# Attention and a graph product on one core: the prelude's copies, scales and keys in another order, and queries split two units ahead

## The chip, the cores and the metric

The kernel runs on one core of a Trainium2 chip. The metric is the device time of one execution in microseconds (us). TensorE multiplies matrices into PSUM (eight banks of 512 float32 in each of 128 partitions), VectorE and ScalarE work element by element, GpSimd and SyncE issue transfers (DMA). Each engine runs its own instructions in order and waits on semaphores.

## The reference

```python
q, k, v = x @ Wq.T + bq, key @ Wk.T + bk, value @ Wv.T + bv      # 4096 x 512 each
scores = (q @ k.T) / 4096 ** 0.5 * adj                           # 4096 x 4096
scores = where(abs(scores) < 1e-5, -1e9, scores)
x1 = layernorm(x + (softmax(scores) @ v) @ Wm.T + bm)
out = layernorm(x1 + relu((adj @ x1) @ W.T + b))
```

## The kernel before

**Numbers.** Products in float32 quality are made of float16 (or float32r) halves: each operand is split into a high half, written by ScalarE, and a low half, what is left, written by VectorE; each product has three passes (high by high, low by high, high by low). Operands are first multiplied by a power of two: `up[:, S_K]` for keys, `up[:, S_V]` for values, `up[:, S_T]` for queries, `up[:, S_W]` for the weights of the values.

**Folding.** q @ k.T is computed as (x A + bq Wk) key.T plus a term for each query row, with A = Wq.T Wk, and Wv and Wm are multiplied into one matrix (Wvm). So "queries" below are t = x A + b, called t, 32 tiles of 128 rows.

**Prelude.** TensorE makes A (L773), the rows of the biases (L756), turns Wm (L787), turns the first rows of x (L765) and multiplies Wv by Wm (L802). ScalarE copies in the order: Wq and Wk, biases, Wv (L1091), A out of PSUM (L1094), Wm. VectorE makes the low halves in the same order (L1350, L1371, L1382), with the rows of the biases (L1375 to L1379) ahead of Wm's. SyncE has loaded Wq and Wk, x's first rows, Wm and Wv; GpSimd issues the loads of 2048 keys (L669) once the last part of Wk is in.

Then come eight groups G of four tiles. For each e of 0 to 3, TensorE turns a tile of x for group G + 1 (`x_turn`, banks 0 and 1), in groups 4 to 6 turns a tile of 128 keys in bank BK = 2 (`key_turn`, L831; the next turn waits for the low half, L1442), and makes 128 columns of the group's queries in bank BT + e, BT = 4 (`queries`, L818). ScalarE writes x's high half (L1075), the key's (L1119) and copies the queries to `tq` (L1113), which GpSimd stores in `t_dram`. VectorE makes the low halves (L1343, L1442), the largest magnitudes of keys and values, one chunk of 512 rows at a time (`chunk_maximum`, L1403; the staging buffers `stg` are loaded anew by GpSimd, L659, when a chunk has been read), and of the queries (`t_maximum`, L1408, `last_t_maximum`, L1414). A scale is made in steps: `scale_square` (L1420, L1423) spreads the maxima of the partitions over a square `gsq`, TensorE turns it (`scale_turn`, L825), and `scale_made` (L1427 to L1438) makes the power of two. S_W is made at the start of group 2, S_K of group 4, S_V of group 6, S_T after group 7. The raw Wvm is split after its scale (L1141, L1473). The last four key tiles (KEYS_AFTER) are turned after group 7, in one bank; VectorE makes their low halves before `scale_made(S_T)`.

**Units.** A unit g is one tile of queries by one half of the keys: 32 units for each half. TensorE makes its scores (`scores`, L857, 48 matmuls in four banks BS + c) and weights the values with its probabilities (`weigh`, L877, 48 matmuls). VectorE adds and masks the scores (L1535, which frees the bank), ScalarE takes magnitudes (L1168), VectorE sets small ones to -1e9 and takes the maximum, ScalarE makes exponentials (L1173) and the high probabilities (L1181), VectorE the low ones (L1564), and SyncE turns both by DMA (L375, L378) into `PT`, which `weigh` reads. The tile of t for unit g + 1 is loaded (`load_t`, L350) and split (`t_high`, L1158; `t_low`, L1508) in the step of unit g, so `scores(g + 1)` waits for it. `thl` has two buffers. The output of a unit of the first half is copied (`copy_first`, L1186) and stored (`store_first`).

The order of TensorE is written out: scores 0, 1, weigh 0, scores 2, weigh 1, scores 3, weigh 2, then loops of scores(g), weigh(g - 1). After the second half's units come products with adj (L972, L1004).

Of the kernel before, what the change touches and what calls it, by code (L numbers as in the profile page):

```python
# [21 lines left out]
P_SCALE = 2.0 ** 14  # L22

# [18 lines left out]
def attention_then_aggregation(nc, x, adj, key, value, wq, bq, wk, bk, wv, bv, wm, bm, w1, b1, out):  # L42
# [40 lines left out]
    with ctx:  # L83
# [10 lines left out]
        tcol = sb(ctx, "tcol", [P, NG + KD - 1], fp32)  # L94
# [101 lines left out]
        with ExitStack() as prep:  # L196
# [9 lines left out]
            bq_k = sb(prep, "bq_k", [P, KD, 1], fp32)  # L206
            bcol = sb(prep, "bcol", [P, 3, KD], fp32)
# [43 lines left out]
        t_mm, t_ev, t_mx = sem("t_mm"), sem("t_copied"), sem("t_maxima")  # L251
# [57 lines left out]
        KEYS_AFTER = (12, 13, 14, 15)  # L309

# [12 lines left out]
        with nc.Block() as block:  # L323

            @block.sync
            def _(sp):
# [44 lines left out]
                def turn_prob(g, b):  # L371

                    scales_made()
# [29 lines left out]
                def first_step(g, b, j):  # L403

                    nb, nj = 1 - b, j + b
                    load_t(g + 1, g + 1)
# [4 lines left out]
                    if not isinstance(g, int) or g >= 1:  # L411
                        store_first(g - 1, g - 1, 1 - b)
# [22 lines left out]
                with sp.Fori(1, NT // 2 - 1) as i:  # L435
                    for b in range(2):
                        first_step(2 * i + b, b, i)
# [4 lines left out]
                load_t(g + 1, 0)  # L442
# [72 lines left out]
                def second_step(n, b, j, merged, rows, products, copied=False, sums=False, copies=False):  # L515

                    g = NT + n
                    if not isinstance(n, int) or n < NT - 1:
                        load_t(g + 1, n + 1)
# [36 lines left out]
                load_t(NT + 1, 1)  # L556
# [86 lines left out]
            def _(pool):  # L643
# [23 lines left out]
                pool.wait_ge(s_w[KD - 1], 32)  # L667
# [84 lines left out]
            def _(pe):  # L752
# [45 lines left out]
                pe.wait_ge(s_rout, 4)  # L798
# [10 lines left out]
                def queries(G, e):  # L809
# [4 lines left out]
                    wait(pe, t_ev, KD * (G - 1) + e + 1)  # L814
# [12 lines left out]
                def key_turn(m):  # L827
                    pe.wait_ge(key_in[m // TC], 16)
                    wait(pe, k_lo, m)
                    for k in range(KD):  # L830
                        last = nc.tensor.transpose(ps[:, BK, k * P:(k + 1) * P], keyn[:, m, k * P:(k + 1) * P], ident[:, :])  # L831
# [86 lines left out]
                scores(1, 1, 0)  # L918
                weigh(0, 0, 0)
                scores(2, 0, 0)  # L920
# [150 lines left out]
            def _(act):  # L1071
# [34 lines left out]
                def t_out(G, e):  # L1106
                    b = G % 2
                    act.wait_ge(t_mm, KD * G + e + 1)
                    if G >= 2:

                        act.wait_ge(t_st[b], 16 * (G // 2))
                        act.wait_ge(t_mx, G - 1)
# [956 lines left out]
```

## Time and profile before

| | before |
|---|---|
| time, median of 3 runs (lowest to highest) | 2096.1 us (2095.8 to 2097.22) |
| the profiled execution: time / span | 2098.29 us / 2096.6 us |
| TensorE busy | 2044.8 us, 98% of the span |
| VectorE / ScalarE / GpSimd busy | 1466.7 / 676.3 / 81.5 us |
| mean share of full TensorE clock granted | 0.989 |
| scores (L857) / weighted values (L877) | 676.5 / 673.5 us |
| the queries' products (L818) | 97.0 us |

The span runs from the first to the last instruction of one profiled execution; the time of that execution also holds what lies around them. A line of the timeline gives start, duration, engine, line of the kernel, operation, out<-in, shapes, and in brackets how long the engine had stood idle before it and what released it.

### The profile page before, as it was taken

How to read it: one execution, taken by the hardware profiler on the slowest of the kernel's cores; microseconds unless marked ns; L12 is line 12 of the kernel's file. 1: busy time of each engine (PE TensorE's matmuls, PEld its weight loads, DVE VectorE, ACT ScalarE, POOL GpSimd, SP SyncE). 2: the span in 40 equal slices, each digit the busy share in tenths (PEclk: the TensorE clock that was granted, in tenths of full speed). 3: DMA queues.
4: the chain of work that ended last, by engine and by line, in shares of the span. 5: the costliest groups of instructions: out<-in, count | busy, mean ns of one | idle time of the engine just before them, and what ended most of it. 6: DMA issues, size and time to landing. Idle time of an engine off the chain costs nothing.

```text
span 2096.6 us, 29772 instructions
## 1 busy us (share of the span) xinstructions
PE 2044.8 (98%) x9471; PEld 980.8 (47%) x9471; DVE 1466.7 (70%) x3354; ACT 676.3 (32%) x884; POOL 81.5 (4%) x139
## 2 busy tenths in 40 slices
PE   7987999999999999999999999999999999999998
PEld 6873444444444444444444444444444444444443
DVE  3876656565666656587777777778888757887887
ACT  3343434343434344343333333334444210000000
POOL 1110000000000000000000000000000000000000
PEclk9998999999999999999999999999999999999999
DMA  7675886767677766788666666777777996455551
GB/s 246 216 281 147 194 184 144 177 154 178 151 174 157 173 158 164 208 177 182 161 160 161 161 162 162 168 171 182 180 180 210 229 266 148 126 121 120 135 134 61
DMA packets 586673, 359.56 MB, mean 171 GB/s; under 512 B 501376, under 2 KB 505472, under 8 KB 586240
## 3 DMA queue, kind: packets, MB, share of 16 engines
q1 hardware_dynamic: 565056, 275.07, 52.5%
q0 software_dynamic: 21568, 83.89, 16.4%
q8 instruction: 24, 0.39, 0.1%
q14 instruction: 25, 0.20, 0.0%
HBM read 181.15 MB, written 88.60 MB: 129 GB/s over the span
## 4 chain that ended last, share of the span: by engine, by line
PE 93%; DVE 3%; DMA 2%; SPq 1%; ACT 1%; issue 0%; DVEq 0%; ACTq 0%
PE ps L857 31%; PE ps L877 31%; PE ps L1004 16%; PE ps L912 4%; PE ps L898 4%; PE ps L818 3%; PE ps L972 2%; DMA wc<-in_L_gnn_Wv 1%; PE ps L802 1%; DMA x1T<-x1hl 1%; PE ps L765 0%; DMA stg<-in_L_gnn_value 0%; PE ps L831 0%; DVE mcol L1403 0%; DVE tcol L1408 0%
## 5 line engine op out<-in xcount | busy, mean ns | idle before, releaser
L857 PE MATMUL ps<-KT,thl 128*128 128x512 f16 x3072 | 676.5, 380 | 9.9 <-DVE thl L1508 9.9
L877 PE MATMUL ps<-V,PT 128*128 128x512 f16 x3072 | 673.5, 379 | 0.6 <-issue 0.6
L857 PEld LDWEIGHTS ps<-KT,thl 128*128 128x128 f16 x3072 | 301.1, 98 | 375.2 <-DVE thl L1508 11.3
L877 PEld LDWEIGHTS ps<-V,PT 128*128 128x128 f16 x3072 | 300.4, 98 | 363.5 <-issue 1.9
L1535 DVE SCALAR_TENSOR_TENSOR prob<-ps,c_now,adjh 128x512 f32<-128x512 f32 x256 | 192.1, 751 | 288.4 <-PE ps L857 287.6
L1168 ACT ACTIVATE small<-prob 128x512 f32<-128x512 f32 x256 | 161.8, 632 | 629.5 <-DVE prob L1535 342.5
L1564 DVE SCALAR_TENSOR_TENSOR Phl<-prob,Phl 128x2048 f16<-128x2048 f32 x64 | 146.7, 2292 | 77.3 <-ACT Phl L1181 77.1
L1548 DVE CUSTOM_DVE_ANT_0 prob<-prob,small 128x512 f32<-128x512 f32 x256 | 174.4, 684 | 0.0
L1173 ACT ACTIVATE prob<-prob,nbias,inv 128x2048 f32<-128x2048 f32 x64 | 134.2, 2097 | 95.1 <-DVE nbias L1557 95.1
L1541 DVE TENSOR_SCALAR small<-small,eps_s,neg_s 128x512 f32<-128x512 f32 x256 | 139.2, 544 | 21.0 <-ACT small L1168 21.0
L1181 ACT ACTIVATE Phl<-prob 128x2048 f16<-128x2048 f32 x64 | 122.4, 1912 | 7.1
L1331 ACT ACTIVATE p<-ps 128x512 f32<-128x512 f32 x14 | 8.4, 598 | 332.1 <-PE ps L1004 332.1
L1004 PE MATMUL ps<-Y,AT 128*128 128x512 f16 x448 | 99.0, 379 | 0.0
L818 PE MATMUL ps<-xT,Aq 128*128 128x512 f32 x384 | 97.0, 403 | 1.8 <-DVE xT L1343 1.8
L912 PE MATMUL ps<-W1T,x1T 128*128 128x512 f16 x384 | 91.3, 389 | 5.3 <-DMA x1T<-x1hl 5.3
L696 POOL DMA_DIRECT2D adjh<-in_adj x64 | 36.3, 568 | 1387.2 <-DMA adj_bf<-adjh 782.5
L898 PE MATMUL ps<-Wvm,UT 128*128 128x512 f16 x384 | 88.1, 379 | 0.2 <-issue 0.2
L1004 PE MATMUL ps<-Ta,S 128*128 128x512 f16 x336 | 79.4, 379 | 0.0
L1004 PE MATMUL ps<-Tb,S 128*128 128x512 f16 x336 | 79.4, 379 | 0.0
L818 PEld LDWEIGHTS ps<-xT,Aq 128*128 128x128 f32 x384 | 71.0, 191 | 16.6 <-DVE xT L1343 2.5
L1004 PEld LDWEIGHTS ps<-Y,AT 128*128 128x128 bf16 x448 | 43.8, 98 | 52.8
L912 PEld LDWEIGHTS ps<-W1T,x1T 128*128 128x128 f16 x384 | 38.2, 100 | 53.3 <-DMA x1T<-x1hl 6.3
(182 smaller groups left out, 1739.7 us busy)
## 6 DMA issues: line engine op xcount, KB each, us to landing
adjh<-in_adj POOLq DMA_DIRECT2D x64, 512.0 KB, 5.4
adj_bf<-adjh SPq DMA_DIRECT2D x64, 512.0 KB, 4.4
t_in<-t_dram SPq DMA_DIRECT2D x64, 256.0 KB, 2.9
x_in<-in_x SPq DMA_DIRECT2D x64, 256.0 KB, 4.2
stg<-in_L_gnn_value POOLq DMA_DIRECT2D x12, 1024.0 KB, 7.2
rows<-in_x SPq DMA_DIRECT2D x32, 256.0 KB, 3.7
t_dram<-tq POOLq DMA_DIRECT2D x8, 1024.0 KB, 8.9
o_dram<-z_out SPq DMA_DIRECT2D x32, 256.0 KB, 2.8
```

The costliest lines, as they stand in the source:

```text
L818: last = nc.tensor.matmul(ps[:, BT + e, :], Aq[:, m, k, e * P:(e + 1) * P], xT[:, b, s, k, :], start=(n == 0), stop=(n == 3 * KD - 1))
L857: last = nc.tensor.matmul(ps[:, BS + c, :], thl[:, b, s, k * P:(k + 1) * P], KT[:, m, k, c * C:(c + 1) * C], start=(n == 0), stop=(n == 3 ...
L877: last = nc.tensor.matmul(ps[:, BU + b, :], PT[:, b, s, m, :], V[:, v, m, :], start=(m == 0 and q == 0), stop=(m == MT - 1 and q == 2))
L898: last = nc.tensor.matmul(ps[:, BZ, :], UT[:, b, s, k, :], Wvm[:, m, k, :], start=(n == 0), stop=(n == 3 * KD - 1))
L912: last = nc.tensor.matmul(ps[:, BY, :].rearrange("p (o n) -> p o n", n=P), x1T[:, s, k, :], W1T[:, m, :, k, :], start=(q == 0), stop=(q == ...
L1004: last = nc.tensor.matmul(ps[:, bank, :].rearrange("p (s d) -> p s d", s=2), left(m), right(m), start=(m == 0), stop=(m == NP - 1))
L1168: nc.scalar.activation(small[:, c % 2, :], prob[:, b, c * C:(c + 1) * C], ACT.Abs).then_inc(s_abs, 1)
L1173: nc.scalar.activation(prob[:, b, :], prob[:, b, :], ACT.Exp, bias=nbias[:, b:b + 1], scale=inv[:, 0:1], accum_out=rsum[:, b:b + 1]).then_ ...
L1535: nc.vector.scalar_tensor_tensor(out=prob[:, b, c * C:(c + 1) * C], in0=ps[:, BS + c, :], scalar=c_now[:, b:b + 1], in1=adjh[:, b, c * C:( ...
L1541: nc.vector.tensor_scalar(small[:, c % 2, :], small[:, c % 2, :], eps_s[:, 0:1], neg_s[:, 0:1], ALU.is_lt, ALU.mult).then_inc(s_neg, 1)
L1548: nc.vector.tensor_tensor_reduce(out=prob[:, b, c * C:(c + 1) * C], in0=prob[:, b, c * C:(c + 1) * C], in1=small[:, c % 2, :], scale=1.0, ...
L1564: nc.vector.scalar_tensor_tensor(out=Phl[:, b, LO, :], in0=prob[:, b, :], scalar=P_SCALE, in1=Phl[:, b, HI, :], op0=ALU.mult, op1=ALU.subt ...
```

## The change

- The sums that make the queries' scale: behind each copy of queries, ScalarE takes the magnitude in place in PSUM, times 2^-9, and sums it over 512 columns into one column of `tcol` (32 columns instead of 11); the maximum of these sums makes the scale, with TOP x 2^-9. The maxima on VectorE are gone. TensorE waits for the sum and not for the copy before it writes the bank again. A second copy of the bias, times 2^-9, is made.
- ScalarE and VectorE take A out of PSUM before they split Wv. GpSimd waits for Wv instead of Wk before it loads keys.
- S_W is made two tiles later (group 2, tile 2), Wvm's high half one tile later, its low half at the start of group 3.
- The last four key tiles are turned into four banks, those of the queries; their low halves are made after the first unit's queries are split.
- A tile of t is loaded and split two units ahead: 0 and 1 at the start, then g + 2 in the step of unit g.
- TensorE makes the scores of units 0, 1 and 2 before it weighs unit 0. ScalarE copies the outputs of 0 and 1 behind its step of unit 2, and SyncE stores them there.

```diff
@@ SyncE
                 def first_step(g, b, j):
-                    load_t(g + 1, g + 1)
+                    load_t(g + 2, (g + 2) % NT if isinstance(g, int) else g + 2)
                     wait(sp, s_c, g)
...
-                    if not isinstance(g, int) or g >= 1:
+                    if isinstance(g, int) and g == 2:
+                        store_first(0, 0, 0)
+                    if not isinstance(g, int) or g >= 2:
                         store_first(g - 1, g - 1, 1 - b)
...
                 load_key(0, 0)
+                load_t(1, 1)
@@ GpSimd
-                pool.wait_ge(s_w[KD - 1], 32)
+                pool.wait_ge(s_wv, 16)
                 for q in range(MC):
                     pool.dma_start(keyn[:, q * TC:(q + 1) * TC, :], chunk(key, q)).then_inc(key_in[q], 16)
@@ TensorE
-                    wait(pe, t_ev, KD * (G - 1) + e + 1)
+                    wait(pe, t_mx, KD * (G - 1) + e + 1)
...
-                    wait(pe, k_lo, m)
+                    if m in KEYS_AFTER:
+                        pe.wait_ge(t_mx, KD * (NG - 1) + m - KEYS_AFTER[0] + 1)
+                    else:
+                        wait(pe, k_lo, m)
...
-                        if e == 0 and G in (2, 4, 6):
+                        if (G, e) in ((2, 2), (4, 0), (6, 0)):
                             scale_turn(G // 2 - 1)
...
                 scores(1, 1, 0)
+                scores(2, 0, 0)
                 weigh(0, 0, 0)
-                scores(2, 0, 0)
                 weigh(1, 1, 0)
@@ ScalarE
+                for d in range(KD):
+                    act.wait_ge(s_amm, d + 1)
+                    nc.scalar.activation(Aq[:, HI, d, :], ps[:, d, :], ACT.Copy, scale=SCALE).then_inc(s_ahi, 1)
                 act.wait_ge(s_wv, 16)
                 for e in range(KD):
                     nc.scalar.activation(wv_s[:, HI, e, :], wc[:, e, :], ACT.Copy).then_inc(s_whi, 1)
-                for d in range(KD):
-                    act.wait_ge(s_amm, d + 1)
-                    nc.scalar.activation(Aq[:, HI, d, :], ps[:, d, :], ACT.Copy, scale=SCALE).then_inc(s_ahi, 1)
...
                                          ACT.Identity, bias=bq_k[:, e, :]).then_inc(t_ev, 1)
+                    act.wait_ge(t_ev, KD * G + e + 1)
+                    nc.scalar.activation(ps[:, BT + e, :], ps[:, BT + e, :], ACT.Abs, bias=bq_d[:, e, :], scale=T_DOWN,
+                                         accum_out=tcol[:, KD * G + e:KD * G + e + 1]).then_inc(t_mx, 1)
...
-                        t_high(g + 1, 1 - b)
+                        t_high(g + 2, b)
@@ VectorE
-                        if G == 2 and e == 3:
+                        if G == 3 and e == 0:
                             dve.wait_ge(s_vhi, 1)
...
-                        if G > 0 and e == 2:
-                            t_maximum(G - 1)
...
-                        if G == NG - 1:
-                            last_t_maximum(e)
-                scale_square(S_T, tcol[:, :], t_mx, NG + KD - 1)
-                for m in KEYS_AFTER:
-                    key_low(m)
-                scale_made(S_T)
+                scale_square(S_T, tcol[:, :], t_mx, NG * KD)
+                scale_made(S_T, top=TOP * T_DOWN)
...
                 t_low(0, 0)
+                for m in KEYS_AFTER:
+                    key_low(m)
                 c_first(0, 0, 0, 0)
+                t_low(1, 1)
                 value_low(3)
...
-                    t_low(g + 1, 1 - b)
+                    t_low(g + 2, b)
```

## Rows read from the trace of the kernel before

**Rows 1.** Waits of TensorE over the span: us in total, times, longest.

```profile
PE ps L857 <- DVE thl L1508: 9.9, 3, 5.5
PE ps L787 <- DVE Aq L1371: 8.2, 1, 8.2
```

**Rows 2.** Timeline of all engines, 0 to 58 us.

```profile
6.20 13.37 PE L773 MATMUL ps<-wk_s,wq_s 128*128 128x512 f32 x48 [6.20 <-DVE wk_s L1350]
...
10.22 3.14 POOL L669 DMA_DIRECT2D keyn<-in_L_gnn_key  x4 [8.48 <-DMA wb<-in_L_gnn_Wk]
...
24.84 0.28 PE L781 MATMUL ps<-bb,ones 128*128 128x4 f32 x2
27.64 2.19 ACT L1091 ACTIVATE wv_s<-wc 128x512 fp32r<-128x512 f32 x4 [13.01 <-DMA wc<-in_L_gnn_Wv]
...
33.34 3.64 PE L787 MATMUL ps<-ident,wd 128*128 128x128 f32 x16 [8.22 <-DVE Aq L1371]
...
37.66 0.69 DVE L1382 TENSOR_TENSOR wmT_s<-ps,wmT_s 128x512 fp32r<-128x512 f32 x1 [0.16 <-ACT wmT_s L1097]
...
38.74 3.02 PE L802 MATMUL ps<-wmT_s,wv_s 128*128 128x512 f32 x12
```

**Rows 3.** TensorE by stretch: us, PE busy, granted clock, DMA share, GB/s.

```profile
10.00:20.00 10.00, 10.00 (x43) 1.00 0.97 335
```

**Rows 4.** Timeline of all engines, groups 2 to 4 of the prelude.

```profile
89.56 2.00 ACT L1141 ACTIVATE Wvm<-wvm_raw,up 128x2048 f16<-128x2048 f32 x1
...
92.69 2.34 DVE L1473 SCALAR_TENSOR_TENSOR Wvm<-wvm_raw,up,Wvm 128x2048 f16<-128x2048 f32 x1
...
95.55 2.28 DVE L1403 TENSOR_REDUCE mcol<-stg 128x1 f32<-128x2048 f32 x1
...
98.12 0.75 POOL L659 DMA_DIRECT2D stg<-in_L_gnn_value  x1 [10.06 <-DVE mcol L1403]
...
105.11 2.29 DVE L1403 TENSOR_REDUCE mcol<-stg 128x1 f32<-128x2048 f32 x1 [1.71 <-DMA stg<-in_L_gnn_value]
...
108.53 0.33 PE L825 MATMUL ps<-ident,gsq 128*128 128x128 f32 x1 [2.62 <-DVE gsq L1423]
```

**Rows 5.** Timeline of all engines, one tile of group 4.

```profile
117.30 0.69 ACT L1113 ACTIVATE tq<-ps,bq_k 128x512 f32<-128x512 f32 x1 [1.87 <-PE ps L818]
...
119.12 0.74 DVE L1442 SCALAR_TENSOR_TENSOR KT<-ps,up,KT 128x512 f16<-128x512 f32 x1
...
121.16 0.60 PE L831 MATMUL ps<-ident,keyn 128*128 128x128 f32 x4
```

**Rows 6.** Timeline of all engines, group 7 and the queries' scale.

```profile
156.94 11.20 PE L818 MATMUL ps<-xT,Aq 128*128 128x512 f32 x48 [1.57 <-DVE xT L1343]
...
178.88 0.28 DVE L1427 TENSOR_REDUCE gm<-ps 128x1 f32<-128x128 f32 x1
...
180.12 0.72 ACT L1158 ACTIVATE thl<-t_in,up 128x512 f16<-128x512 f32 x1 [1.95 <-DVE inv L1499]
```

**Rows 7.** Timeline of all engines, the first two units.

```profile
200.49 0.19 ACT L1173 ACTIVATION_READ_ACCUMULATOR prob<-prob,nbias,inv 128x1 f32 x1
...
204.93 0.74 DVE L1535 SCALAR_TENSOR_TENSOR prob<-ps,c_now,adjh 128x512 f32<-128x512 f32 x1
...
220.00 2.29 DVE L1564 SCALAR_TENSOR_TENSOR Phl<-prob,Phl 128x2048 f16<-128x2048 f32 x1 [1.77 <-ACT Phl L1181]
```

**Rows 8.** Timeline of TensorE alone, the first units.

```profile
181.75 12.14 PE L857 MATMUL ps<-KT,thl 128*128 128x512 f16 x48 [4.09 <-DVE thl L1508]
199.36 11.87 PE L857 MATMUL ps<-KT,thl 128*128 128x512 f16 x48 [5.47 <-DVE thl L1508]
211.16 10.52 PE L877 MATMUL ps<-V,PT 128*128 128x512 f16 x48
221.52 10.52 PE L857 MATMUL ps<-KT,thl 128*128 128x512 f16 x48
```

**Rows 9.** DMA of tile PT until 240 us, from issue to landing.

```profile
DMA to landing us min/median/max: 5.7/6.1/6.2
```

More of the change, by code:

```diff
@@ L22 @@
 P_SCALE = 2.0 ** 14
+T_DOWN = 2.0 ** -9
 X_UP = 2.0 ** 9
@@ L309, in attention_then_aggregation, with key_bank @@
         KEYS_AFTER = (12, 13, 14, 15)
+        def key_bank(m):
+            return BT + m - KEYS_AFTER[0] if m in KEYS_AFTER else BK
         def staged(use):
@@ L371, in turn_prob @@
                 def turn_prob(g, b):
+                    if not isinstance(g, int):
+                        sp.to_reg(g + 1)
                     scales_made()
@@ L434, in _ @@
                 sp.dma_start(w1_raw[:, :, :], w1.rearrange("(o p) e -> p o e", p=P)).then_inc(s_wm, 16)
-                with sp.Fori(1, NT // 2 - 1) as i:
+                for b in range(2):
+                    first_step(2 + b, b, 1)
+                with sp.Fori(2, NT // 2 - 1) as i:
                     for b in range(2):
@@ L517, in second_step @@
                     g = NT + n
-                    if not isinstance(n, int) or n < NT - 1:
-                        load_t(g + 1, n + 1)
+                    if not isinstance(n, int) or n < NT - 2:
+                        load_t(g + 2, n + 2)
                     store_adj(g, n, b, j, 1)
@@ L828, in key_turn @@
                     pe.wait_ge(key_in[m // TC], 16)
[L829 removed]
+                    if m in KEYS_AFTER:
+                        pe.wait_ge(t_mx, KD * (NG - 1) + m - KEYS_AFTER[0] + 1)
+                    else:
+                        wait(pe, k_lo, m)
                     for k in range(KD):
[L831 removed]
+                        last = nc.tensor.transpose(ps[:, key_bank(m), k * P:(k + 1) * P], keyn[:, m, k * P:(k + 1) * P], ident[:, :])
                     last.then_inc(k_tr, 1)
@@ L1138, in _ @@
                         t_out(G, e)
-                        if G == 2 and e == 2:
+                        if G == 2 and e == 3:
                             act.wait_ge(s_scaled, S_W + 1)
@@ L1276, in _ @@
                 first_step(0, 0, 0, False, True)
-                first_step(1, 1, 0, True, True)
-                for b in range(2):
-                    first_step(2 + b, b, 1, True, True)
+                first_step(1, 1, 0, False, True)
+                first_step(2, 0, 1, False, True)
+                copy_first(0, 0, 0)
+                copy_first(1, 1, 0)
+                first_step(3, 1, 1, True, True)
                 with act.Fori(2, NT // 2) as i:
@@ L1302, in _ @@
                         second_step(NT + 2 * i + b, b, NT // 2 + i, True, True, True, True, copy=True, kept=True, sums=True)
-                second_step(2 * NT - 2, 0, NT - 1, True, True, True, True, copy=True, kept=True, sums=True)
+                second_step(2 * NT - 2, 0, NT - 1, True, False, True, True, copy=True, kept=True, sums=True)
                 second_step(2 * NT - 1, 1, NT - 1, True, False, True, True, sums=True)
@@ L1366, in _ @@
                     last.then_inc(s_rep, 1)
-                for e in range(KD):
-                    raw_split(wv_s, wc, e, 2 * KD + e + 1)
                 for d in range(KD):
@@ L1373, in _ @@
                                                    op1=ALU.subtract).then_inc(s_alo, 1)
+                for e in range(KD):
+                    raw_split(wv_s, wc, e, 2 * KD + e + 1)
                 dve.wait_ge(s_rmm, 3)
@@ L1423, in scale_square, with scale_made @@
                     nc.vector.tensor_scalar(gsq[:, :], ones[:, :], mx[:, k:k + 1], None, ALU.mult).then_inc(s_gsq, 1)
-                def scale_made(k, bank=BM):
+                def scale_made(k, bank=BM, top=TOP):
                     dve.wait_ge(s_gtr, k + 1)
@@ L1436, in scale_made @@
                     dve.wait_ge(s_gm, 4 * k + 4)
-                    nc.vector.tensor_scalar(down[:, k:k + 1], down[:, k:k + 1], 1.0 / TOP, None, ALU.mult)
-                    nc.vector.tensor_scalar(up[:, k:k + 1], up[:, k:k + 1], TOP / 2, None, ALU.mult).then_inc(s_scaled, 1)
+                    nc.vector.tensor_scalar(down[:, k:k + 1], down[:, k:k + 1], 1.0 / top, None, ALU.mult)
+                    nc.vector.tensor_scalar(up[:, k:k + 1], up[:, k:k + 1], top / 2, None, ALU.mult).then_inc(s_scaled, 1)
                 def key_low(m):
@@ L1466, in _ @@
                             x_out(G + 1, e)
-                        if e == 0 and G in (2, 4, 6):
+                        if (G, e) in ((2, 2), (4, 0), (6, 0)):
                             scale_made(G // 2 - 1)
@@ L1753, in second_step @@
                     maximum(g, b, n, 1)
-                    if nxt:
-                        t_low(g + 1, 1 - b)
+                    if nxt and not (isinstance(n, int) and n == NT - 2):
+                        t_low(g + 2, b)
                     if merging:
```

30 lines of the change are left out of this document (12 added, 18 removed).

## The prediction

> **What bounds the kernel now.** I read the busy shares first: TensorE is busy 98% of the span, so only its idle time and the time in which its clock is down can be won. The waits of TensorE say where that is: one wait for the split A, 8.2 us, and three for the split queries, 9.9 us with 5.5 the longest [rows 1]. Then the timeline: all waits that the change touches lie before 222 us. From there on scores and weighted sums follow one another every 10.36 us with no gap (211.16 to 221.52) [rows 8], which the change leaves as it is. So the question is how much earlier TensorE comes to the fourth unit's scores, at 242.24 = 221.52 + 2 x 10.36. In five stretches:
>
> **1. A out of PSUM before Wv; keys loaded after Wv.** The last product of the bias ends at 25.12 (24.84 + 0.28). TensorE then stands until 33.34, since A's copy is queued behind Wv's on ScalarE and VectorE, and Wv lands at 27.6 [rows 2]. A's own products end at 19.57 (6.20 + 13.37). With the copy first, the two engines have A out some 1.4 us later, at 21, under the bias products, so Wm's transposes begin at 25.1. What is late next is VectorE: between 25.2 and Wv's products it has two instructions of the bias rows and four low halves of Wm, all of the size that took 0.69, and short ones, 0.4 together, one of them new (a second copy of the bias). 25.2 + 6 x 0.69 + 0.4 gives 29.7 where the row of before says 38.74 [rows 2]: **9.0**. The cover is Wv being there by about 22.5, because its split still stands ahead of the bias rows on VectorE. GpSimd's 6 MB of keys no longer start at 10.22, so up to then the queues carry x's first rows, Wm, Wv and a bias, 3.3 MB behind the other weights; at the 335 GB/s of that stretch [rows 3] that is 9.7 us, so Wv lands near 20. Ends: 7.5 to 9.5, or 4 if Wv stays late (rival 3). The keys then land near 36 to 38, and VectorE reads the first only behind Wv's products, 29.7 + 4 x 3.02 = 41.8 [rows 2].
>
> **2. Magnitudes on ScalarE in place of maxima on VectorE.** Seven reduces of 2.28 and four of 0.69 go, 18.7 us of VectorE, none of it ahead of TensorE but at 156. For it ScalarE gets 32 instructions, one behind each copy of 512 query columns. No row shows one that both reads and writes PSUM with a sum. The nearest is the copy itself, 0.69, and the read of the accumulator, 0.19 [rows 5, 7]; with the wait for its own copy I take 0.93. The ends are 0.6 and 2.3 (the exponential over 2048 columns takes 2.1 with its sum). The TensorE of the next group waits for it only a group later. But the next rows of x and the keys queue behind it on ScalarE. In the stretch with keys the copy starts at 117.30, the low key is out at 119.86, and the bank is wanted at 121.16 [rows 5]: 1.30 of slack, 0.37 less the overlap left after 0.93. In groups 4 and 5 VectorE has 0.69 + 0.75 + 2.28 per tile, about TensorE's step of 3.64, so lateness isn't won back there. I charge **-1.0** for the twelve tiles with keys; ends 0 and -6.
>
> The Trainium skill (ScalarE: Activation LUTs, Rules for kernel authors) says to use VectorE and not ScalarE for simple arithmetic, which speaks against the move. By its figure of 280 ns + 0.833 ns a column for one pointer operand the instruction is an estimated 0.71, and the row's 0.69 agrees; its rule of choice would matter only if ScalarE were the late engine.
>
> **3. Weights of the value product, split later.** Now ScalarE's Wvm (2.0) stands at 89.56, VectorE's at 92.69, and the maximum of staged chunk 8 begins at 95.55, which ends at 97.8 and lets GpSimd load the buffer anew at 98.12; it lands 7.0 us later, at 105.11, and behind that maximum are the last rows of x for group 4 and the square of the keys' scale, which TensorE gets at 108.53 [rows 4]. After the change the high Wvm comes one tile later and behind the new magnitude: copy at 92.2, magnitude to 93.6, Wvm to 95.6, then x's rows to 96.2, VectorE's low rows to 96.9, low Wvm to 99.1, chunk 8 to 101.4. The reload is issued at 101.7, lands at 108.7, chunk 10's maximum ends at 111.0, and rows and square (1.2) bring TensorE to 112.2: **-3.6**. Ends: 0, if the reload takes less, and -5. It has no cover; it is on the path now.
>
> The Trainium skill (DMA: Bandwidth & Descriptors, Anatomy of one DMA — SWDGE (gpsimd) path) fits such a transfer as 2.0 us + bytes/436 KB per us, an estimated 4.4 for this one. The row says 7.0, so the trace disagrees; by that fit the loss would be 1.0 and not 3.6.
>
> **4. Group 6 and the scale of the queries.** In group 6 the maximum of group 5 is gone from ahead of the low V, so x's last rows are out at 155.8 and not at 156.9, where TensorE stood 1.57 [rows 6], though ScalarE is 0.9 later each tile: **+1.1**, ends 0 and 1.5. From there, counted in times of before: queries end 166.8, the last copy at 167.7, its magnitude 168.6, square 169.1, turned 169.5, the scale 1.24 later (178.88 to 180.12). The last keys no longer go one by one through a bank, since each has its own, freed by the magnitudes; three are turned at 167 to 168 and the last at 168.7. ScalarE copies four high keys, 168.6 to 171.0, then the high queries to 171.7, VectorE the low ones, 0.8: scores begin at 172.55. That is 16.75 after the queries of group 7 began; before it was 24.81 (156.94 to 181.75) [rows 6, 8]. So **+8.0**, ends 7 and 8.5. The four low keys and V's last part wait behind the low queries on VectorE: keys done at 175.2, before the fourth bank of scores asks for the last. The low V to 179.4 delays the first mask by 2.2, with slack until the second unit's scores.
>
> **5. Three units of scores first, queries two ahead.** Before, from the first scores to the fourth unit's: 17.61 (with the wait of 5.5) + 11.80 + 3 x 10.36 = 60.5 [rows 8]. Afterwards queries 1 are split at 177.2 and queries 2 at 190.3, both before they are wanted, so the waits of rows 1 go. The work is 12.14 + 4 x 10.36 = 53.6. What is late next: scores of unit 2 overwrite the banks of unit 1, whose first mask stands behind unit 0's low probabilities on VectorE, as the mask at 204.93 did, 23.2 after the first scores [rows 7]. That is 195.75, and with the mask 196.5, where TensorE is ready at 195.0: 1.5 lost. The second: unit 1's low probabilities end 17.4 after that mask begins (204.93 to 222.29) [rows 7], and the turned tile lands 5.7 to 6.2 later [rows 9], or sooner since later ones do: some 218.7 against 217.3, 1.4. So 56.5, **+4.0**; ends 2 and 6.5. The extra load of queries on SyncE lies ahead of the stores' waits in an idle queue. In the loop each step loads and splits one tile as before, of a later unit, so it costs nothing; only SyncE gets a register instruction. Stores of the first two outputs now wait for unit 1's sum ahead of a key's turn, which nothing needs for 10 us.
>
> **The sum**, against the profiled execution: 9.0 - 1.0 - 3.6 + 1.1 + 8.0 + 4.0 = 17.5. Its span of 2096.6 becomes 2079.1, and its time, 1.7 more, 2080.8. The median shown is 2.2 below that execution: 2096.1 - 17.5 = **2078.6 us**. Scores after a pause took 12.14 where 10.52 is usual [rows 8]; I keep one such loss before the first scores and one in group 4, as before.
>
> **The rivals.**
> 1. ScalarE sets the pace of the prelude. For: slack of 0.37 a tile at most. Against: 0.69 and 0.19 are in the rows. If the magnitude costs 1.2 to 1.5, some 24 tiles lose 0.15 to 0.3 more: 2082 to 2086.
> 2. Hardly a new stall at the keys' scale: VectorE is ready for the reload at 104.8, so each us that it lands sooner than 108.7, as the queues are emptier, is won, down to 3.1 after its issue. Against: the row's 7.0. If it lands within 4 us, 2078.6 - 3 = 2075 to 2076.
> 3. The first part doesn't do what it says: Wv still lands at 27, because x, Wm and Wv fill the queues. Then VectorE ends Wv's split at 30.2, the bias rows and Wm follow, and Wv's products begin near 34.7: a gain of 4 and not 9, 2083.6. Against: the 335 GB/s held mostly for keys.
> 4. Slower: the magnitude, in place in PSUM with its sum, costs 2.3, the upper end. Then each of some 28 tiles loses 2.3 - 0.93 - 0.3 = 1.07, 30 us, against 17.5 won: 2108. It decides from about 1.85 a magnitude. It would show as TensorE waiting for xT and KT in every tile.
>
> **How the numbers follow.** Forecast 0.55, rival 1 0.2, rival 2 0.12, rival 3 0.06, rival 4 0.03, and 0.04 for several of the losing ends together, within 0.2%. A difference of 0.2% (4 us) is about what a measurement of this kernel can tell from none. The range reaches from 2073 (rival 2 with the better ends of part 5) to 2086 (rival 1's end). Faster 0.93, same 0.04, slower 0.03.
>
> **What would show it.** Wm's transposes start near 25 and Wv's products near 29.7; no wait of TensorE for Aq. The magnitude's row reads near 0.69 with 0.19 behind it. TensorE waits for the keys' gsq 3 to 4 us longer than 2.6 [rows 4], until about 103. The first scores begin near 168 (172.55 - 9.0 + 3.6 + 1.0), with no wait for thl at the second and third. Fourth unit's scores near 225, and 10.36 per product after. It is wrong if steps after that aren't 10.36, if TensorE waits for xT in most tiles, or if Wv lands after 23.

## The result, and the profile after

| | before | after |
|---|---|---|
| time, median (lowest to highest), 4 runs each | 2096.66 us (2095.8 to 2099.06) | 2079.8 us (2077.57 to 2080.16) |
| ratio, 95% interval | | 0.9916 [0.9898, 0.9933] |
| the profiled execution: time / span | 2098.29 / 2096.6 us | 2080.16 / 2078.5 us |
| mean share of full TensorE clock | 0.989 | 0.994 |

16.9 us less by the medians and 18.1 by the spans, where 17.5 was forecast; the interval of the ratio lies wholly below 1. The medians in this document leave out one execution of 2720.68 us of the changed kernel (granted clock 0.744) and one of 5967.63 us of the kernel before. The waits of TensorE in the changed kernel (us in total, times, longest):

```profile
PE ps L930 <- DMA x1T<-x1hl: 6.2, 2, 3.4
PE ps L788 <- DVE wk_s L1373: 6.2, 1, 6.2
PE ps L840 <- DVE gsq L1437: 6.1, 1, 6.1
PE ps L875 <- DVE thl L1516: 2.9, 1, 2.9
PE ps L849 <- DVE KT L1456: 2.0, 3, 1.4
PE ps L875 <- DVE prob L1546: 1.6, 1, 1.6
PE ps L895 <- DMA PT<-Phl: 0.7, 1, 0.7
```

Of the 18.1 us of [rows 1] the 8.2 for A are gone and 2.9 of 9.9 are left for the split queries; the wait for the keys' scale grew from 2.6 [rows 4] to 6.1, and prob and PT are new. The waits for the turned keys (KT) are not new: there were five of them, 7.1 us, and three with 2.0 are left. Three of the five, 5.8 us, were the last keys, one by one through their bank after group 7 of the kernel before:

```profile
PE ps L831 <- DVE KT L1442: 7.1, 5, 2.5
...
171.12 0.85 PE L831 MATMUL ps<-ident,keyn 128*128 128x128 f32 x4 [2.53 <-DVE KT L1442]
173.62 1.09 PE L831 MATMUL ps<-ident,keyn 128*128 128x128 f32 x4 [1.65 <-DVE KT L1442]
176.36 1.09 PE L831 MATMUL ps<-ident,keyn 128*128 128x128 f32 x4 [1.66 <-DVE KT L1442]
```

Line numbers have shifted: L787 is now L802 (Wm's transposes), L802 L817 (Wv's products), L825 L840 (turns of a scale), L831 L849 (turns of keys), L818 L833 (queries), L857 L875 (scores), L877 L895 (weighted values). The timeline of all engines in the changed kernel, around Wv and A:

```profile
6.17 13.50 PE L788 MATMUL ps<-wk_s,wq_s 128*128 128x512 f32 x48 [6.17 <-DVE wk_s L1373]
17.67 2.64 ACT L1109 ACTIVATE Aq<-ps 128x512 fp32r<-128x512 f32 x4 [2.60 <-PE ps L788]
20.50 2.19 ACT L1112 ACTIVATE wv_s<-wc 128x512 fp32r<-128x512 f32 x4 [0.19 <-DMA wc<-in_L_gnn_Wv]
20.77 3.14 POOL L684 DMA_DIRECT2D keyn<-in_L_gnn_key  x4 [19.04 <-DMA wc<-in_L_gnn_Wv]
...
24.95 0.28 PE L796 MATMUL ps<-bb,ones 128*128 128x4 f32 x2
25.09 1.95 PE L802 MATMUL ps<-ident,wd 128*128 128x128 f32 x16
...
29.48 2.97 PE L817 MATMUL ps<-wmT_s,wv_s 128*128 128x512 f32 x12 [0.33 <-DVE bq_d L1411]
```

It answers [rows 2]: A is being copied while its last products run, Wv lands at 20.5 and not at 27.6, Wm's transposes follow the bias without a gap, and Wv's products begin at 29.48 and not at 38.74. The same view at the keys' scale, which answers [rows 4]:

```profile
84.30 1.99 ACT L1161 ACTIVATE Wvm<-wvm_raw,up 128x2048 f16<-128x2048 f32 x1
87.42 2.34 DVE L1487 SCALAR_TENSOR_TENSOR Wvm<-wvm_raw,up,Wvm 128x2048 f16<-128x2048 f32 x1
89.67 2.28 DVE L1428 TENSOR_REDUCE mcol<-stg 128x1 f32<-128x2048 f32 x1
92.25 0.75 POOL L674 DMA_DIRECT2D stg<-in_L_gnn_value  x1 [13.12 <-DVE mcol L1428]
99.25 2.29 DVE L1428 TENSOR_REDUCE mcol<-stg 128x1 f32<-128x2048 f32 x1 [3.91 <-DMA stg<-in_L_gnn_value]
102.66 0.47 PE L840 MATMUL ps<-ident,gsq 128*128 128x128 f32 x1 [6.13 <-DVE gsq L1437]
```

VectorE stood 3.91 us for the reload of the staging buffer, which again was there 7.0 after its issue (92.25 to 99.25). The view of all engines at one tile of group 4 (it answers [rows 5]) and at the queries' scale ([rows 6]):

```profile
111.75 0.69 ACT L1130 ACTIVATE tq<-ps,bq_k 128x512 f32<-128x512 f32 x1 [1.06 <-PE ps L833]
112.47 0.66 ACT L1134 ACTIVATE ps<-ps,bq_d 128x512 f32<-128x512 f32 x1
113.05 0.19 ACT L1134 ACTIVATION_READ_ACCUMULATOR ps<-ps,bq_d 128x1 f32 x1
113.14 0.59 ACT L1093 ACTIVATE xT<-ps 128x512 fp32r<-128x512 f32 x1
...
147.67 13.90 PE L833 MATMUL ps<-xT,Aq 128*128 128x512 f32 x60
161.40 1.48 PE L849 MATMUL ps<-ident,keyn 128*128 128x128 f32 x12
...
163.25 0.63 PE L849 MATMUL ps<-ident,keyn 128*128 128x128 f32 x4 [0.37 <-ACT ps L1134]
...
165.32 0.72 ACT L1178 ACTIVATE thl<-t_in,up 128x512 f16<-128x512 f32 x1
```

The magnitude takes 0.66, and reading its sum 0.19. Three keys are turned (x12) while the last queries are copied, the fourth 1.85 later, and between that and the high queries stands only the scale. TensorE alone over the first units, as in [rows 8]:

```profile
166.95 22.58 PE L875 MATMUL ps<-KT,thl 128*128 128x512 f16 x96 [2.93 <-DVE thl L1516]
191.09 10.52 PE L875 MATMUL ps<-KT,thl 128*128 128x512 f16 x48 [1.56 <-DVE prob L1546]
201.45 10.52 PE L895 MATMUL ps<-V,PT 128*128 128x512 f16 x48
212.65 10.52 PE L895 MATMUL ps<-V,PT 128*128 128x512 f16 x48 [0.68 <-DMA PT<-Phl]
223.00 10.52 PE L875 MATMUL ps<-KT,thl 128*128 128x512 f16 x48
```

From there on each product takes 10.36, as before. Between marks that both traces have (us):

| stretch, to this mark of TensorE | before | after | saved | forecast |
|---|---|---|---|---|
| start of Wv's products | 38.74 | 29.48 | 9.26 | 9.0 |
| turn of the keys' scale | 69.79 | 73.18 | -3.39 | -3.6 |
| end of group 7's queries | 59.61 | 58.91 | 0.70 | 1.1 - 1.0 |
| first scores | 13.61 | 5.38 | 8.23 | 8.0 |
| fourth unit's scores | 60.49 | 56.05 | 4.44 | 4.0 |
| end of the span | 1854.4 | 1855.5 | -1.1 | 0 |

(The first row is a start; each row below it is the stretch from the mark above. The twelve tiles with keys, for which 1.0 was charged, lie in groups 4 to 6, all behind the keys' scale. The queries of group 7 end at 168.14 = 156.94 + 11.20 before, and at 161.57 = 147.67 + 13.90 after.)

### The profile page after: what moved, and what is told of

Read it like the earlier page. It is cut to its first block, busy times and chain, and to the rows that moved or that the text cites. A ratio compares the mean times of both kernels' runs of the same rounds, so it can differ in the third digit from the quotient of the medians.

```text
span 2078.5 us, 29826 instructions
## 1 busy us (share of the span) xinstructions
PE 2041.1 (98%) x9471; PEld 978.0 (47%) x9471; DVE 1449.1 (70%) x3344; ACT 698.9 (34%) x948; POOL 81.0 (4%) x139
## 4 chain that ended last, share of the span: by engine, by line
PE 94%; DMA 2%; DVE 2%; ACT 1%; SPq 1%; issue 0%; DVEq 0%; ACTq 0%
PE ps L895 31%; PE ps L875 31%; PE ps L1022 16%; PE ps L930 4%; PE ps L916 4%; PE ps L833 3%; PE ps L990 2%; DMA stg<-in_L_gnn_value 1%; PE ps L788 1%; DMA x1T<-x1hl 1%; PE ps L817 1%; DVE mcol L1428 0%; PE ps L771 0%; PE ps L780 0%; SPq L384 0%
## 5 line engine op out<-in xcount | busy, mean ns | idle before, releaser
L875 PE MATMUL ps<-KT,thl 128*128 128x512 f16 x3072 | 675.0, 380 | 4.5 <-DVE thl L1516 2.9
L895 PE MATMUL ps<-V,PT 128*128 128x512 f16 x3072 | 673.5, 379 | 0.9 <-DMA PT<-Phl 0.7
L875 PEld LDWEIGHTS ps<-KT,thl 128*128 128x128 f16 x3072 | 300.8, 98 | 368.4 <-issue 4.3
L895 PEld LDWEIGHTS ps<-V,PT 128*128 128x128 f16 x3072 | 300.3, 98 | 364.0 <-issue 2.3
L833 PE MATMUL ps<-xT,Aq 128*128 128x512 f32 x384 | 96.5, 402 | 0.0
L833 PEld LDWEIGHTS ps<-xT,Aq 128*128 128x128 f32 x384 | 71.1, 191 | 14.2
```

What stands on the lines that cost most here:

```text
L833: last = nc.tensor.matmul(ps[:, BT + e, :], Aq[:, m, k, e * P:(e + 1) * P], xT[:, b, s, k, :], start=(n == 0), stop=(n == 3 * KD - 1))
L875: last = nc.tensor.matmul(ps[:, BS + c, :], thl[:, b, s, k * P:(k + 1) * P], KT[:, m, k, c * C:(c + 1) * C], start=(n == 0), stop=(n == 3 ...
L895: last = nc.tensor.matmul(ps[:, BU + b, :], PT[:, b, s, m, :], V[:, v, m, :], start=(m == 0 and q == 0), stop=(m == MT - 1 and q == 2))
```

## The experiments

The theory was that each stretch gained by its own edit, as the prediction priced it. Each run below undoes or alters one edit of the changed kernel. What it did is read between marks, since the first products of A begin and run a little differently in each execution. Two kernels were profiled twice (below), and that shows how far a single execution can be trusted. From Wv's products to the fourth unit's scores the changed kernel took 193.52 and 193.51 us, but its stretches in between differed by up to 0.6; the kernel with Wvm early took 190.71 and 192.28. The stretch to the keys' scale repeated best, within 0.15 in both. For the rest, a difference of up to some 1.6 us between single executions counts here only where a wait in the trace shows it, and the column of single times tells little by itself: the changed kernel's own lie between 2077.03 and 2081.74.

| kernel | Wv's products | to keys' scale | to first scores | to fourth unit's | time |
|---|---|---|---|---|---|
| changed | 29.48 | 73.18 | 64.29 | 56.05 | 2080.16 |
| changed, second execution | 29.71 | 73.33 | 63.69 | 56.49 | 2077.03 |
| keys early | 33.54 | 74.75 | 63.52 | 56.47 | 2082.38 |
| Wv first | 28.54 | 73.25 | 65.25 | 58.05 | 2082.08 |
| two scores first | 28.66 | 73.42 | 64.67 | 61.94 | 2085.27 |
| Wvm early | 29.08 | 70.53 | 64.39 | 55.79 | 2075.92 |
| Wvm early, second execution | 28.95 | 70.64 | 65.60 | 56.04 | 2076.75 |
| two magnitudes | 29.66 | 74.88 | 70.13 | 55.45 | 2087.01 |
| maxima on VectorE | 30.07 | 72.47 | 66.40 | 56.42 | 2081.62 |
| keys through one bank | 30.15 | 73.13 | 72.52 | 56.00 | 2088.06 |

(Start of Wv's products, then the length of each stretch, and the time of that one execution, in us.)

**Keys loaded as early as before.**

```diff
@@ GpSimd
-                pool.wait_ge(s_wv, 16)
+                pool.wait_ge(s_w[KD - 1], 32)
```

> The changed kernel, but GpSimd starts the keys' loads after Wk again, not after Wv. Theory (the keys held Wv back; the order of A and Wv is only half of part 1): Wv lands near 27, VectorE ends its split at about 30, the bias rows and Wm follow, Wv's products begin at 34 to 35 and not at 29.5; span and time 5 us longer than the changed kernel, 2085. Rival (the order of the copies alone carries it): Wv's products begin at 29.5 and the time stays at 2080.

**Wv split ahead of A, as before; keys late.**

```diff
@@ ScalarE
-                for d in range(KD):
-                    act.wait_ge(s_amm, d + 1)
-                    nc.scalar.activation(Aq[:, HI, d, :], ps[:, d, :], ACT.Copy, scale=SCALE).then_inc(s_ahi, 1)
                 act.wait_ge(s_wv, 16)
                 for e in range(KD):
                     nc.scalar.activation(wv_s[:, HI, e, :], wc[:, e, :], ACT.Copy).then_inc(s_whi, 1)
+                for d in range(KD):
+                    act.wait_ge(s_amm, d + 1)
+                    nc.scalar.activation(Aq[:, HI, d, :], ps[:, d, :], ACT.Copy, scale=SCALE).then_inc(s_ahi, 1)
@@ VectorE
+                for e in range(KD):
+                    raw_split(wv_s, wc, e, 2 * KD + e + 1)
                 for d in range(KD):
                     dve.wait_ge(s_ahi, d + 1)
...
-                for e in range(KD):
-                    raw_split(wv_s, wc, e, 2 * KD + e + 1)
```

> The changed kernel, but both engines split Wv before they take A out of PSUM, as before; the keys still wait for Wv. Theory (Wv lands at 20.5 without the keys beside it, so its split costs little ahead of A): A is out near 25.7, Wm's transposes begin at 25.8, Wv's products at about 30.1, time 0.6 us over the changed kernel, 2080.5. Rival (the order carries it): Wm's transposes begin at 28 or later and the time is 2083 or more.

TensorE with the keys early:

```profile
30.53 1.12 PE L806 MATMUL ps<-ident,xu 128*128 128x128 f32 x4 [4.42 <-DVE bb L1400]
33.54 4.42 PE L817 MATMUL ps<-wmT_s,wv_s 128*128 128x512 f32 x12
```

and with Wv first:

```profile
28.54 3.01 PE L817 MATMUL ps<-wmT_s,wv_s 128*128 128x512 f32 x12 [0.33 <-DVE bq_d L1411]
```

From the end of A's products to Wv's: 19.17 before (38.74 - 19.57), 14.79 with A first alone (33.54 - 18.75), 9.82 with the late keys alone (28.54 - 18.72), 9.81 with both (29.48 - 19.67). So the order alone is worth 4.4, the late keys alone 9.35, and the order adds nothing once the keys are late: with Wv first, Wv's products began at 28.54, and not at the 30.1 that I expected. The wait of 4.42 for the bias is rival 3 as it was described: Wv landed at 26.0 in that kernel, and VectorE stands at Wv's split with the bias rows behind it. (Behind Wv's products, Wv first lost 3.0 more: 1.4 at the keys and 1.3 in the first scores, at a lower clock. Whether that comes of the order, one execution doesn't tell; so "nothing" holds for the stretch up to Wv's products, and what the order does to the whole is not shown.)

**Two units of scores first, queries still two ahead.**

```diff
@@ TensorE
-                scores(2, 0, 0)
                 weigh(0, 0, 0)
+                scores(2, 0, 0)
                 weigh(1, 1, 0)
```

> The changed kernel, but TensorE weighs unit 0 before the scores of unit 2, as before; queries stay split two ahead. Theory (the wait for thl covered a wait for PT): the second scores follow the first without a gap, but weighing unit 0 then waits some 6 us for PT, whose low half is made at 190.2 and lands about 5 later; the fourth unit's scores begin at 226.6 and not 223.0, time 2083.4, so that splitting two ahead alone is worth next to nothing of the 5.5. Rival (the wait for thl was the whole stall): fourth scores at 223 or earlier, time 2080.

TensorE in this kernel:

```profile
166.75 22.29 PE L875 MATMUL ps<-KT,thl 128*128 128x512 f16 x96 [2.92 <-DVE thl L1516]
194.99 13.14 PE L895 MATMUL ps<-V,PT 128*128 128x512 f16 x48 [5.95 <-issue]
```

61.94 to the fourth unit's scores, where the kernel before needs 60.49: splitting two ahead, alone, gains nothing. The waits for split queries come back as one of 5.95 for the first weights. The line puts it down to "issue"; the view of tile PT names it as TensorE's wait for the turned probabilities of unit 0, whose last DMA is issued near 190.6. The products after it take 13.14 and not 10.52, at a granted clock of 0.84 from 190 to 212 us. I expected the wait (6) but not that: the fourth unit's scores began at 228.69 and not at 226.6. The gain of part 5 is the third unit of scores, which fills that wait; without queries split two ahead it couldn't run there, so the two edits of part 5 only work together.

**The first high and low Wvm as early as before.**

```diff
@@ TensorE and VectorE
-                        if (G, e) in ((2, 2), (4, 0), (6, 0)):
+                        if (G, e) in ((2, 0), (4, 0), (6, 0)):
@@ ScalarE
-                        if G == 2 and e == 3:
+                        if G == 2 and e == 2:
@@ VectorE
-                        if G == 3 and e == 0:
+                        if G == 2 and e == 3:
```

> The changed kernel with Wvm's scale and its two halves back at their places of before (scale at the start of group 2, high half at its third tile, low half at its fourth). Theory (the later low half holds chunk 8's maximum, and so the reload of the buffer for chunk 10, back): TensorE waits about 1.3 for x's rows at the start of group 3, chunk 8 starts near 87.2 and not 89.7, the wait for the keys' square falls from 6.1 to about 2.5, its end comes 2.4 earlier, the fourth unit's scores begin near 220.6 and the time is 2077.5. Rival (the magnitudes on ScalarE are what is late there): the square comes at 102.7 as in the changed kernel or later, time 2080 or more.

TensorE in this kernel:

```profile
83.96 3.06 PE L833 MATMUL ps<-xT,Aq 128*128 128x512 f32 x12 [1.06 <-DVE xT L1366]
99.61 0.33 PE L840 MATMUL ps<-ident,gsq 128*128 128x128 f32 x1 [2.55 <-DVE gsq L1437]
```

The wait for the keys' scale is back at 2.55, the stretch to it 2.65 shorter (70.53 against 73.18), and 1.06 of the gain is paid for x's low rows at 83.96. Of the -3.39, 2.65 are this edit. The other 0.7 comes with the magnitudes: the kernel without them (maxima on VectorE, 72.47) is 0.7 shorter up to the keys' scale than the changed one. Both kernels were timed again beside one another on one chip:

> The changed kernel once more, beside the next run on the same chip. 2079 to 2081, ratio to the kernel before 0.991 to 0.992; fourth unit's scores 193 to 194 us behind the start of Wv's products.

2079.6 us (2077.03 to 2081.74, four executions), ratio to before 0.9914 [0.9897, 0.9932].

> The same kernel as the one with Wvm split as early as before, now timed beside the changed kernel on one chip. If the 2.8 us that its stages gained in one look are real: 2076 to 2078, some 3 below the changed kernel, ratio to the kernel before 0.990 to 0.991. If that look was luck: as the changed kernel, 2079 to 2081.

2077.3 us (2076.75 to 2077.86), ratio 0.9901 [0.9885, 0.9917]: 2.3 less than the changed kernel beside it. The intervals overlap, but all four runs of this kernel lie below three of the four of the changed one, and both profiled executions have the shorter stretch. The second had the keys' scale 70.64 after Wv's products, but gained 1.2 in all up to the fourth unit and not 2.8: with it came a wait of 0.98 for a key at 125.28 that the first profiled execution did not have. So the 2.7 up to the keys' scale are shown twice, and that the whole kernel is faster is likely but not shown.

**Two magnitudes per tile in place of one** (the second in place once more, its sum unread).

```diff
@@ ScalarE
+                    act.wait_ge(t_mx, 2 * (KD * G + e) + 1)
+                    nc.scalar.activation(ps[:, BT + e, :], ps[:, BT + e, :], ACT.Abs, bias=bq_d[:, e, :], scale=T_DOWN,
+                                         accum_out=tcol2[:, KD * G + e:KD * G + e + 1]).then_inc(t_mx, 1)
```

> The changed kernel with every magnitude made twice, the second one in place over the first with its sum into columns that nobody reads; its output is not the reference's concern, as only the first sum makes the scale. It prices the slack under the magnitudes. Theory (a slack of 0.2 to 0.5 a tile is left after the first): each of 28 tiles loses 0.9 - 0.3 = 0.6, 17 us, time near 2096, with TensorE waiting for xT and KT in every tile. Rival (TensorE isn't bound by ScalarE even so): under 5 us, time under 2085.

TensorE's waits up to 300 us in this kernel:

```profile
PE ps L841 <- DVE gsq L1441: 7.0, 2, 6.4
...
PE ps L850 <- DVE KT L1460: 3.3, 5, 2.1
...
PE ps L850 <- ACT ps L1138: 2.7, 2, 1.6
```

I expected a loss of 17 us, and named under 5 as the rival; neither came. Here the second magnitude starts 0.81 after the first, 26 us of ScalarE over 32 tiles, and TensorE is 6.9 later at the fourth unit (74.88 + 70.13 + 55.45 = 200.46 after Wv's products, and 193.52 in the changed kernel). 1.7 of it lies ahead of the keys' scale, 5.8 between it and the first scores. Thus ScalarE does set the pace with a second one, mostly with keys beside it, but a tile absorbs far more than the 0.3 that I took from one tile's row: 26 us of work cost 6.9.

**Maxima on VectorE again, the four banks kept.** The edit puts back the seven reduces of 2.28 and four of 0.69 and takes the magnitudes out.

```diff
@@ ScalarE
-                    nc.scalar.activation(ps[:, BT + e, :], ps[:, BT + e, :], ACT.Abs, bias=bq_d[:, e, :], scale=T_DOWN,
-                                         accum_out=tcol[:, KD * G + e:KD * G + e + 1]).then_inc(t_mx, 1)
@@ VectorE
+                        if G > 0 and e == 2:
+                            t_maximum(G - 1)
...
+                        if G == NG - 1:
+                            last_t_maximum(e)
```

> The changed kernel with the magnitudes gone from ScalarE and the maxima back on VectorE, as before (scale from maxima); the last keys keep their four banks, freed by the copies. Theory (the move of the work is worth little in itself: VectorE's maxima lie where it idles, but for one in group 6 ahead of a value's low half): the wait for the square stays near 6, group 6 loses about 1 and groups 4 and 5 win as much or less, the scores' start after group 7 is unchanged within 0.3; time 2079.5 to 2081.5. Rival (the move carries a good part of the gain): 2083 or more.

The one new wait of TensorE is ahead of group 7, as in [rows 6]:

```profile
152.28 11.18 PE L833 MATMUL ps<-xT,Aq 128*128 128x512 f32 x48 [1.60 <-DVE xT L1364]
```

195.29 against 193.52 up to the fourth unit. The difference of 1.8 is hardly more than two executions of one kernel can differ by, but 1.6 of it is this wait, which stood at the same place in the kernel before (1.57 [rows 6]) and in no execution of the changed kernel. So the move to ScalarE is worth about 1.6. The reduces, 18.7 us of VectorE's time, cost TensorE no more than that.

**The last four keys through one bank**, and with it their low halves ahead of the queries' scale again; the edit undoes both.

```diff
-                    return BT + m - KEYS_AFTER[0] if m in KEYS_AFTER else BK
+                    return BK
@@ VectorE
                 t_low(0, 0)
-                for m in KEYS_AFTER:
-                    key_low(m)
...
+                for m in KEYS_AFTER:
+                    key_low(m)
                 scale_made(S_T, top=TOP * T_DOWN)
```

> The changed kernel with the last four keys turned in one bank, their low halves made ahead of the queries' scale, as before. Theory (the chain turn, high, low of each key, 2.6 to 2.7 us, was the tail before): the four turns take 8 us after group 7 and not 2.5, the first scores begin near 173.6 and not 166.95, time 2086.5. Rival (the earlier square is what counts): first scores before 169, time 2082 or less.

TensorE in this kernel:

```profile
165.22 0.80 PE L846 MATMUL ps<-ident,keyn 128*128 128x128 f32 x4 [2.61 <-DVE KT L1453]
167.67 1.08 PE L846 MATMUL ps<-ident,keyn 128*128 128x128 f32 x4 [1.66 <-DVE KT L1453]
170.41 1.08 PE L846 MATMUL ps<-ident,keyn 128*128 128x128 f32 x4 [1.66 <-DVE KT L1453]
175.80 22.55 PE L872 MATMUL ps<-KT,thl 128*128 128x512 f16 x96 [4.09 <-DVE thl L1515]
```

The stretch to the first scores is 8.2 longer, and the parts before and after it are unchanged. So the four banks, with the low halves moved behind the first unit's queries, carry the whole of part 4's 8.2. How it divides between the two, no run tells; 5.9 of it are the three waits for KT, and the wait for thl is 4.09 and not 2.93.

**Further on from the changed kernel.** Can the wait for the keys' scale go altogether, if one staged chunk less stands ahead of it?

```diff
@@ VectorE
-                IN_GROUP = {0: (0, 1, 2, 3), 1: (4, 5), 2: (6, 7), 3: (8, 9, 10), 4: (11, 12, 13), 5: (14, 15)}
+                IN_GROUP = {0: (0, 1, 2, 3), 1: (4, 5), 2: (6, 7), 3: (8, 9), 4: (10, 11, 12), 5: (13, 14, 15)}
```

> The changed kernel with the maximum of staged chunk 10 and all behind it one place later: chunk 10 in group 4 (with 11 and 12), 13 to 15 in group 5. Theory (the 6.1 us wait for the keys' square is chunk 10's load, which stands ahead of x's last rows and of the square on VectorE and which the keys' scale doesn't need): the square is ready at about 96.5 and not 102.7, the clock loss of 1.6 behind the wait goes too, and 2 to 3 us come back as waits for KT in group 4, as chunks 11 and 12 now stand beside the first keys; time 2073 to 2076. Rival (the loads' pace is the bound, wherever the chunks stand): the wait moves into group 4 and 5 whole, time 2079 to 2081.

It went, but waits for keys came in its place. TensorE up to 300 us:

```profile
PE ps L849 <- DVE KT L1456: 6.7, 6, 1.4
...
PE ps L840 <- DVE gsq L1437: 0.9, 1, 0.9
```

The stretch to the scale is 6.2 shorter (66.94), the next 4.5 longer (68.83). 2078.29 us (2078.03 to 2078.44), ratio 0.9904 [0.9888, 0.9921], where I expected 2073 to 2076; by the intervals it can't be told from the changed kernel. Two more kernels went after those waits: the first twelve keys alternate between two banks, and then, besides, the low Wvm stands behind the keys' square.

```diff
-                    return BT + m - KEYS_AFTER[0] if m in KEYS_AFTER else BK
+                    return BT + m - KEYS_AFTER[0] if m in KEYS_AFTER else BK + m % 2
...
-                        wait(pe, k_lo, m)
+                        wait(pe, k_lo, m if m in (1, 9) else m - 1)
```

> The kernel with chunk 10 later, and besides keys 0 to 11 turned in two banks by turns (2 and 3, the second shared with the scales' turns), so that a key's turn waits for the low half of the key before the last. Theory (with chunk 10 later TensorE waits 6.7 us in six places for KT, which one more bank hides, while x's rows have two banks already): the waits for KT fall under 2 us in all, fourth unit's scores near 217, time 2073 to 2075. Rival (the staged loads set the pace of groups 4 and 5, since x's low rows stand behind the maxima too): TensorE waits for xT instead of KT by as much, time 2077 to 2078.

```diff
@@ VectorE
-                        if G == 3 and e == 0:
+                        if G == 3 and e == KD - 1:
```

> The same, and the low half of Wvm moved on VectorE from the start of group 3 to its end, behind the square of the keys' scale, where VectorE idles 1.8 us. Theory (chunk 8 then ends 2.3 earlier and with it all reloads up to chunk 11): the short wait for xT in group 3 goes, chunk 11 no longer waits for its load, 0.3 to 1.5 us less than with Wvm's low half early, time 2072 to 2074. Rival (nothing waits for these loads any more once the keys have two banks): the same time within 0.3.

The first took the waits for KT to 1.0 and was 190.24 from Wv's products to the fourth unit in its profiled execution, but its runs scatter from 2075.83 to 2084.5 us (median 2080.52, ratio 0.9917 [0.9892, 0.9942]), so it shows no gain, where I expected 2073 to 2075. The second: 2075.07 us (2074.86 to 2078.79), ratio 0.9888 [0.9871, 0.9904]. Its median is the lowest of all that was timed more than once, though its interval too overlaps that of the changed kernel, and I expected 2072 to 2074. Its profile is of its slowest run (192.10 between the marks), with 3.56 lost in one wait for x's rows ahead of group 7 (at 147.46), so where the other runs gained is not shown.

## Why the prediction was right

- **Part 1 (9.0, measured 9.26).** The sum was right, its cause only half right. I took the order of A and Wv as the carrier and the late keys as its cover. The late keys are worth 9.35 alone, the order nothing beside them. Wv landed at 20.5, as worked out (near 20). Rival 3's mechanism is real, 14.79 against 9.81 with early keys; only its condition wasn't met.
- **Parts 2 and 3 (-1.0, -3.6, +1.1; measured -3.39 and 0.70).** The magnitude took 0.66 and 0.19, and the wait of 1.57 ahead of group 7 is gone, against 1.1 forecast. Of the charge of 1.0 for the tiles with keys, 0.7 shows: in groups 4 to 6 TensorE waited 1.3 for keys before (0.71 and 0.58) and 2.0 after, 1.4 of it once, in group 6, where the high V stands ahead of a key on ScalarE. That would make 0.9, and 0.70 was measured; for the 0.2 I have no row. The stall at the keys' scale came as traced, step by step: reload issued at 92.25, 7.0 to land, TensorE at 102.66 where "about 103" was forecast; the kernel with Wvm early bears out the cause for 2.65 of the 3.39. The other 0.7 comes with the magnitudes: without them (72.47) this stretch is 0.7 shorter. Part 3 had that too, with the magnitude worked in ahead of the high Wvm.
- The Trainium skill (DMA: Bandwidth & Descriptors, Anatomy of one DMA — SWDGE (gpsimd) path) would have had the reload in an estimated 4.4 us, and with it a loss of 1.0. It took 7.0 again, the queues at 235 GB/s together from 85 to 105 us; the trace disagrees, and rival 2, which lived on a sooner landing, falls with it.
- **Part 4 (8.0, measured 8.23).** Three keys turned at once, the last 1.85 later, high queries 0.72, all as worked out. The run with one bank and the low halves in front gives the size back, 8.2.
- **Part 5 (4.0, measured 4.44).** The third unit's scores began 24.14 after the first, where the mask on VectorE was reckoned at 23.95 (196.5 - 172.55). The turned tile was waited for 0.68 and not 1.4 (1.11 in the second execution), where tiles landed 4.3 to 5.5 us after their issue (median 4.5), and 5.7 to 6.2 was taken from [rows 9]: that term was mis-sized, and it is what part 5 gained over the forecast in this execution.
- **The rest (0, measured -1.1).** In the changed kernel's second profiled execution the stretch behind the fourth unit's scores took 1852.1 and not 1855.5, with 1854.4 before: it scatters by 3.4 from one execution to the next. Part of that shows at TensorE's waits near the end for x1T, the turned x1 of the last products (5.3 before, 6.2 and 5.6 after); the rest of it no wait accounts for. It is no effect of the change that these runs can show.
- **Rivals 1 and 4** didn't come about, since the magnitude had the cost of its nearest rows; no run tested one of 1.2 or 2.3. The run with two magnitudes says that their price for a late ScalarE was too high: 0.81 more on ScalarE in every tile costs 6.9 us, less than half of what the slack of 0.3 in each of 28 tiles would leave uncovered (0.81 - 0.3, and 14). A slack read from one tile of a tight group isn't the slack of all: 5.8 of the 6.9 came in the groups behind the keys' scale, where keys pass through ScalarE too.
- The sum held with terms off by 0.2 to 0.6, all on the good side (1.7 together), and the rest of the program, off by 1.1 the other way, took most of that back. That the total came within 0.6 is in so far luck; that each stretch came within 0.6 is not.

## What to carry to other kernels

Price a reordering by the stretch between two marks that it can't move (here Wv's products, the keys' scale, the first and the fourth scores), profile one kernel twice to see how far the marks repeat, and undo edits one by one: of two edits aimed at one wait, one may carry all of it. When a step is moved to a later slot of an engine, follow what it delays there up to the next buffer that a load waits for; the low Wvm, made later just ahead of a maximum, cost 2.7 us up to the keys' scale through a buffer that it never touches. Read a slack in every kind of tile before you multiply it by their number.

## What the runs showed of the hardware

- Six megabytes of loads on GpSimd's queue, issued from 10.22 on, held back Wv, queued on its own: it landed at 27.6 with them beside it and at 20.5 without, though the rate was near the same (335 and 321 GB/s from 10 to 20 us). With the keys early again but A first it landed at 26.0, 16.6 after its issue, and TensorE waited 4.4 for the bias rows behind its split. So I read the 7 us as shared bandwidth; the runs show the delay, not how the queues share.
- The granted clock, as shares of 2.4 GHz, in the same stretch before and after (us, PE busy, clock, DMA share, GB/s):

```profile
165.00:185.00 20.00, 10.06 (x39) 0.66 0.69 194
```

```profile
165.00:185.00 20.00, 18.05 (x76) 0.91 0.59 148
```

  A gap ahead of products can cost twice: before, TensorE was idle half of this stretch and the clock stood partly at the lower of its two levels (1.2 and 2.4 GHz), and 48 products took 12.14, where 10.52 is usual [rows 8]. After the changed kernel's wait of 2.93 the first 96 took 22.58, and behind the same wait 23.86 with Wv split first (a clock of 0.83 in this stretch); but in the second execution with Wvm early, behind the same wait of 2.93:

```profile
165.19 20.89 PE L875 MATMUL ps<-KT,thl 128*128 128x512 f16 x96 [2.93 <-DVE thl L1516]
188.93 10.52 PE L875 MATMUL ps<-KT,thl 128*128 128x512 f16 x48 [2.84 <-DVE prob L1546]
```

  There the clock held (1.00 from 165 to 185 us), and only 0.4 was won (23.74 from first to third unit's scores, against 24.14): the wait for the mask grew from 1.56 to 2.84, since VectorE, not TensorE, sets when the third unit may begin. The kernel with the keys in two banks shows the same pair, 20.89 and a wait of 2.82.
